# A unit of token work on TensorE ahead of the sums of the step before, in a two-layer attention kernel

## Chip, cores and metric

The kernel runs on 1 core of one Trainium2 chip. The metric is device time in microseconds (us); the time before is a median of 3 runs.

## The reference

What is computed is a chain of two transformer layers on x of shape (4, 1024, 128), all in fp32, each sublayer with a residual and a layernorm without weights behind it:

- layer 0: attention with 16 heads of 8, q and k normalised over the whole row of 128 and divided by sqrt(8), scores divided by a temperature per head, softmax over all 1024 keys, projection with bias; then a linear layer with inputs quantised to int8 per row.
- layer 1: attention with 16 heads of 8, a layernorm per head on q and k, rotary embedding, a causal mask, softmax, projection with bias; then a gated MLP with 384 hidden units: down(silu(gate) * up).

```python
attn = softmax(q @ k.T / temperature); out = (attn @ v) @ proj_w.T + proj_b
x = layernorm(x + out)
x = layernorm(x + quantised_matmul(x, weight_q) * weight_scale + bias)
scores = where(tril, scale * q @ k.T, -inf); out = softmax(scores) @ v @ Wo.T + bo
x = layernorm(x + out)
x = layernorm(x + (silu(x @ wg.T) * (x @ wu.T)) @ wd.T)
```

## The kernel before, in words

The queries are cut into 8 chunks of 512 tokens (4 batches, two halves) per layer. A pass is one chunk and one group of 4 heads; there are 64 passes, two passes make a pair, and the 4 passes (two pairs) of a chunk together fill `attn`. A pass is cut into steps of 128 keys (`STEPS`, 400 of them; in layer 1 keys behind the mask are left out and remainders of two passes share a step).

In every step the attention engines do this:

- TensorE, scores (`scores`, L885): two blocks of 2 heads each, transposed scores of 128 keys by 512 queries; each block fills two banks of `ps`. There are three such slots, so block k waits until ScalarE has read block k-3.
- ScalarE (L757): an exponential of each block into `probs` (128x1024). GpSimd zeroes what the causal mask takes (L673, `mask`).
- TensorE, sums (`sums`, L907): probs times v, all four heads side by side in bank `ACC`, together with a row of ones that gives the denominators. They accumulate over both passes of a pair.
- at the end of a pair VectorE turns the bank (`whole_chunk`, "turn": L1151, L1154, L1155) into `heads_t`; at the end of a chunk it transposes `heads_t` into `attn` (L1158).

Beside it runs the token work: everything of the layers that isn't attention, cut into pieces. Its TensorE pieces are the *units*: `qkv` (L853), `qkT` and `normT` and `xqT` (transposes, L779), `ffn` (L848), `proj` (L838), `gate` and `up` (L860), `down` (L864). All write the one bank `SIDE` (`stage`), and VectorE reads each (`read`) before the next may start. A unit also waits for its own input: `proj` for `attn` (`attn_ready`), others for results of VectorE. The VectorE pieces stand between the reads. A planner (`side_order`) that runs when the kernel is built writes for every step which unit and which VectorE pieces belong to it (`SIDE_ORDER`); at most one unit stands in a step, 200 of the 202 units stand in steps that this change can touch. The planner estimates TensorE's and VectorE's time with fixed prices and supposes that the unit comes behind the sums, except in the pending steps (below). `proj` stands 3 steps behind the last step of its chunk.

TensorE's order in step s (`steps` in the TensorE block, L960 on) is: scores of blocks 2s+3 and 2s+4, then the sums of step s-1, then the unit of step s. TensorE executes in program order. One kind of step is different, the *pending* step: if step s-1 is the first of a pair, its sums overwrite the bank that VectorE is turning, so the unit goes first and these sums come behind it. The step before it (s-1 is the last of a pair) holds the sums that the turn waits for.

SyncE issues the DMAs (parts of q and k out to `parts_scratch`, L540; rows back into `q_st` and `k_st`, L522) in an order of its own that comes from the same schedule; GpSimd copies v into `v_st` (L655). ScalarE also does a tanh for each gate unit, two steps behind it.

Of the kernel before, what the change touches and what calls it, by code (L numbers as in the profile page):

```python
# [85 lines left out]
STEPS = []  # L86
# [6 lines left out]
STEPS = [(*x, FIRST[x[0]] == s, LAST_STEP[x[0]] == s) for s, x in enumerate(STEPS)]  # L93
# [271 lines left out]
def program(nc, a, ctx):  # L365
# [408 lines left out]
    def _(pe):  # L774
# [93 lines left out]
        def scores(k, shifted):  # L868

            s, tiles_ = k // 2, STEPS[k // 2][1]  # L870
            for p in dict.fromkeys(x[0] for x in tiles_):
                if k % 2 == 0 and FIRST[p] == s:
                    pe.wait_ge(rows_in[p % KB], 32 * (p // KB + 1) + (32 * PRODUCTS - 32 if p % KB == 0 else 0))
                    if shifted:
                        shifts(p)
            if k % 2 == 0 and tiles_[0][0:2] == (0, TC):
                pe.wait_ge(more_rows_in, 16 * PRODUCTS)
            if k >= SLOTS:

                pe.wait_ge(probs_ready, k - SLOTS + 1)  # L880
            for p, kt, lo, at, n in tiles_:
                for e in range(2):
                    h = k % 2 * 2 + e
                    row = slice(h * HR, (h + 1) * HR)
                    last_ = mm(slot(k)[:, e, at:at + n], k_st[row, p % KB, kt * P:(kt + 1) * P],  # L885
                               q_st[row, p % KB, lo:HALF], start=True, stop=not shifted)
                    if shifted:
                        row = slice(h * HR, h * HR + PARTS)
                        last_ = mm(slot(k)[:, e, at:at + n], ones_st[row, :], shift_st[row, p % 2, lo:HALF], start=False, stop=True)
            last_.then_inc(scores_ready, 1)  # L890

        def sums(s):
            _, tiles_, w, m, _, _ = STEPS[s]
            for p in dict.fromkeys(x[0] for x in tiles_):
                if FIRST[p] == s:
                    pe.wait_ge(v_in, p + 1)
                    if p and p % 2 == 0:
                        pe.wait_ge(sums_turned, p // 2)
            if tiles_[0][0:2] == (0, TC):
                pe.wait_ge(more_v_in, 1)  # L900
            if m:
                pe.wait_ge(masked, MASKED[s])
            else:
                pe.wait_ge(probs_ready, 2 * s + 2)
            for x, (p, kt, lo, at, n) in enumerate(tiles_):
                for h in range(GH):
                    last_ = mm(acc[HR * h:HR * (h + 1), lo:HALF], v_st[:, p % VB, kt, h, :],  # L907
                               probs[:, (2 * s + h // 2) % PS, h % 2, at:at + n], start=FIRST[p] == s and p % 2 == 0 and x == 0,
                               stop=LAST_STEP[p] == s and p % 2 == 1 and x == len(tiles_) - 1, skip_group_check=True)
            last_.then_inc(sums_ready, 1)  # L910
# [25 lines left out]
        def keep_warm(n, bank):  # L936
            for _ in range(n):
                mm(ps[:, bank, :], warm[:, 0:P], warm[:], start=True, stop=True)
# [21 lines left out]
        def steps(shifted):  # L960
            if shifted:
                for name, c, e, what, k in FIRST_KEYS:
                    if e == "pe":
                        stage(name, c, what, k)

            pe.wait_ge(parts_ready["prep"], 2)
            for k in range(SLOTS):
                scores(k, shifted)
            if not shifted:
                stage("prep", 1, "qkT", 1)  # L970
            for s in range(NS + 1):
                for k in (2 * s + 3, 2 * s + 4):
                    if k < 2 * NS:
                        scores(k, shifted)
                if s < 2 and not shifted:
                    keep_warm(WARM[4], ACC)
                pending = s > 1 and STEPS[s - 1][4] and STEPS[s - 1][0] % 2 == 0
                if s and not pending:
                    sums(s - 1)
                for name, c, e, what, k in SIDE_ORDER[s]:  # L980
                    if e == "pe" and (name, c, e, what, k) != FIRST_KEYS[0] and \
                            not (shifted and (name, c, e, what, k) in FIRST_KEYS):
                        stage(name, c, what, k)
                if s and pending:

                    sums(s - 1)
            end()

        with pe.If(far_scores < 1):
            steps(False)  # L990
        with pe.Else():
            steps(True)
# [437 lines left out]
```

## Time and profile before

| | |
|---|---|
| median of 3 runs | 862.54 us (862.50 to 862.57) |
| the profiled execution's own time | 866.08 us |
| its span, first to last instruction | 864.4 us |
| granted TensorE clock, mean | 0.989 |
| TensorE, ScalarE, VectorE, GpSimd busy | 96%, 89%, 64%, 17% |
| HBM | 51.0 MB read, 35.7 MB written |

The profile's records are of one execution. PE is TensorE's matmuls, PEld its weight loads, ACT ScalarE, DVE VectorE, POOL GpSimd, SPq SyncE's DMA issues; L with a number is a line of the kernel. A matmul's recorded end is modelled, and consecutive matmuls overlap, so lengths on TensorE are best read from start to start.

### The profile page before, as it was taken

Reading aid. Unit: us, or ns where it says so; the run is one execution under the profiler, and the core shown is the slowest. Engines: PE = TensorE matmul, PEld = TensorE weight load, DVE = VectorE, ACT = ScalarE, POOL = GpSimd, SP = SyncE. Lnnn points to the kernel's source line nnn. Section 1 sums busy time; section 2 is a strip of 40 time slices with the busy share of each in tenths; the row PEclk is TensorE's granted clock in tenths of the full one; section 3 lists DMA queues with packets and bytes.
Section 4 is the critical chain, followed back from the end, with each engine's and each line's share of the span. In section 5 each row is a group of like instructions: output and inputs, shape, how many; then the busy total and the mean of one; then the engine's idle time right before and its main releaser. Section 6 shows DMA issues by size and latency. Waiting matters only on the chain.

```text
span 864.4 us, 16509 instructions
## 1 busy us (share of the span) xinstructions
PE 831.2 (96%) x6266; PEld 307.4 (36%) x6268; DVE 550.9 (64%) x1459; ACT 771.8 (89%) x864; POOL 150.1 (17%) x352
## 2 busy tenths in 40 slices
PE   8899999999999899999999999999999999989995
PEld 4232333333333333333333433343333443434444
DVE  6264666668758567787672576765563476765656
ACT  4899999999999799899899999999999998979851
POOL 3000000000001400034100410023200442352210
PEclk9999999999999899999999999999999999989998
DMA  5755513314432611352340321142140330062000
GB/s 152 246 160 184 171 38 115 105 37 158 161 122 76 218 38 61 111 184 74 134 160 25 111 98 38 61 160 74 38 159 25 98 112 25 26 221 85 1 13 27
DMA packets 48565, 88.60 MB, mean 103 GB/s; under 512 B 5088, under 2 KB 14432, under 8 KB 48480
## 3 DMA queue, kind: packets, MB, share of 16 engines
q1 hardware_dynamic: 48000, 87.00, 29.9%
q8 instruction: 52, 0.85, 0.4%
q10 hardware_dynamic: 480, 0.48, 0.2%
q14 instruction: 33, 0.27, 0.1%
HBM read 51.03 MB, written 35.65 MB: 100 GB/s over the span
## 4 chain that ended last, share of the span: by engine, by line
PE 80%; DVE 11%; DMA 3%; issue 3%; SPq 2%; ACT 1%; POOL 1%; DVEq 0%; ACTq 0%; POOLq 0%
PE ps L907 39%; PE ps L885 24%; PE ps L853 5%; PE ps L864 3%; PE ps L860 3%; PE ps L779 3%; DMA q_st<-parts_scratch 2%; PE ps L838 2%; ACT probs L757 1%; DVE th L1310 1%; DVE hT L1311 1%; SPq L540 1%; DVE sums_t L1151 1%; DVE mid_part L1300 1%; DVE mid_part L1301 1%
## 5 line engine op out<-in xcount | busy, mean ns | idle before, releaser
L757 ACT ACTIVATE probs<-ps 128x1024 f32<-128x1024 f32 x800 | 751.7, 1073 | 58.3 <-PE ps L885 55.6
L907 PE MATMUL ps<-probs,v_st 128*32 128x512 f32 (+3 forms) x3584 | 430.4, 562 | 3.4 <-issue 1.2
L885 PE MATMUL ps<-q_st,k_st 32*128 32x512 f32 (+3 forms) x1792 | 269.7, 462 | 7.8 <-DMA q_st<-parts_scratch 5.2
L885 PEld LDWEIGHTS ps<-q_st,k_st 32*128 32x128 f32 x1792 | 123.7, 184 | 251.1 <-ACT probs L757 157.4
L673 POOL TENSOR_SCALAR_AFFINE_SELECT probs<-probs 128x256 f32<-128x256 f32 x256 | 108.6, 444 | 152.1 <-ACT probs L757 150.7
L907 PEld LDWEIGHTS ps<-probs,v_st 128*32 128x32 f32 x3584 | 76.4, 109 | 112.1 <-issue 79.3
L655 POOL COPY v_st<-v_all 128x256 f32<-128x256 f32 (+1 forms) x65 | 28.3, 437 | 404.4 <-PE ps L907 396.5
L1151 DVE STREAM_TRANSPOSE sums_t<-ps 128x512 f32<-128x512 f32 x32 | 22.9, 716 | 44.0 <-PE ps L907 43.5
L1285 DVE COPY mid_qkv<-ps 128x384 f32<-128x384 f32 x32 | 17.8, 558 | 38.4 <-PE ps L853 35.6
L860 PE MATMUL ps<-yTp,w_hid 128*128 128x512 f32 x84 | 30.8, 448 | 4.4 <-DVE hT L1311 1.5
L1285 DVE COPY prep_qkv<-ps 128x384 f32<-128x384 f32 x24 | 13.4, 558 | 30.9 <-PE ps L853 30.8
L853 PE MATMUL ps<-w_qkv,yT 128*128 128x384 f32 x64 | 29.2, 538 | 0.0
L864 PEld LDWEIGHTS ps<-w_down,hT 128*128 128x128 f32 x168 | 20.8, 191 | 23.3 <-issue 16.5
L1262 DVE TENSOR_TENSOR x_all<-ps,x_all 128x512 f32<-128x512 f32 x15 | 10.4, 692 | 26.9 <-PE ps L838 26.9
L864 PE MATMUL ps<-w_down,hT 128*128 128x128 f32 x168 | 26.2, 292 | 1.2 <-DVE last_y L1315 0.8
L1305 DVE COPY gate_sb<-ps 128x512 f32<-128x512 f32 x21 | 14.5, 691 | 18.6 <-PE ps L860 18.5
L1315 DVE TENSOR_TENSOR last_y<-ps,last_y 128x128 f32<-128x128 f32 x24 | 7.0, 292 | 30.0 <-PE ps L864 29.7
L860 PEld LDWEIGHTS ps<-yTp,w_hid 128*128 128x128 f32 x84 | 12.5, 188 | 35.2 <-issue 12.8
L1310 DVE SCALAR_TENSOR_TENSOR th<-th,gate_sb 128x512 f32<-128x512 f32 x21 | 14.7, 701 | 15.9 <-PE ps L860 15.6
L853 PE MATMUL ps<-w_qkv,xT 128*128 128x384 f32 x48 | 21.9, 538 | 0.7
L1300 DVE CAST mid_part<-ps 128x512 fp32r<-128x512 f32 x18 | 12.4, 692 | 15.2 <-PE ps L779 14.1
L838 PE MATMUL ps<-w_out,attn 128*128 128x128 f32 x120 | 17.2, 286 | 2.8 <-DVE attn L1158 2.6
(188 smaller groups left out, 634.0 us busy)
## 6 DMA issues: line engine op xcount, KB each, us to landing
k_st<-parts_scratch SPq DMA_DIRECT2D x47, 512.0 KB, 3.5
parts_scratch<-mid_part SPq DMA_DIRECT2D x36, 512.0 KB, 3.9
q_st<-parts_scratch SPq DMA_DIRECT2D x63, 256.0 KB, 4.2
parts_scratch<-prep_part SPq DMA_DIRECT2D x28, 512.0 KB, 4.0
k_st<-parts_scratch SPq DMA_DIRECT2D x16, 256.0 KB, 2.8
xT<-in_xT SPq DMA_DIRECT2D x8, 256.0 KB, 5.0
x_all<-in_x SPq DMA_DIRECT2D x8, 256.0 KB, 5.6
out<-yo SPq DMA_DIRECT2D x7, 256.0 KB, 2.4
```

What stands on the lines that cost most here:

```text
L655: return g_.tensor_copy(v_st[:, p % VB, t, :, p % 2 * SR:p % 2 * SR + D], v_all[:, layer, b % 2, t, g * GH * D:(g + 1) * GH * D] .rearrang ...
L673: op = g_.affine_select(out=block_, in_=block_, compare_op=ALU.is_ge, fill=0.0, base=0, pattern=[[0, 2], [1, P]], channel_multiplier=-1)
L757: nc.scalar.activation(probs[:, k % PS, :, 0:w], slot(k)[:, :, 0:w], ACT.Exp).then_inc(probs_ready, 1)
L779: last_ = tp(dst[:, t * P:(t + 1) * P], src(t), idn[:])
L838: last_ = mm(side[:, t * P:(t + 1) * P], attn[:, t * P:(t + 1) * P], w_out[:, layer, :], start=True, stop=True)
L853: last_ = mm(side[:, 0:3 * C], src[:, k * P:(k + 1) * P], w_qkv[:, 0 if name == "prep" else 1, :], start=True, stop=True)
L860: last_ = mm(side, w_hid[:, 0 if what == "gate" else 1, k * P:(k + 1) * P], yTp[:, n, :], start=(n == 0), stop=(n == PARTS - 1))
L864: last_ = mm(side[:, k * P:(k + 1) * P], hT[:, j, k * P:(k + 1) * P], w_down[:, j * P:(j + 1) * P], start=(j == 0), stop=(j == NJ - 1))
L885: last_ = mm(slot(k)[:, e, at:at + n], k_st[row, p % KB, kt * P:(kt + 1) * P], q_st[row, p % KB, lo:HALF], start=True, stop=not shifted)
L907: last_ = mm(acc[HR * h:HR * (h + 1), lo:HALF], v_st[:, p % VB, kt, h, :], probs[:, (2 * s + h // 2) % PS, h % 2, at:at + n], start=FIRST[ ...
L1151: v.transpose(sums_t[:], acc).then_inc(sums_turned, 1)
L1285: v.tensor_copy(job[name]["qkv"][:, k, :], side[:, 0:3 * C]).then_inc(side_read, 1)
```

## The change

Only the order in TensorE's steps changes. Before, the sums of step s-1 went ahead of the unit, except in a pending step. Now the unit goes ahead of the sums, except where step s-1 is the last of a pair (`STEPS[..][5]` is set for the last step of a pass, and the pass number is odd), and in step 1. The pending steps keep the order that they had. The planner, with its supposition on the order, and the lists of all other engines stay as they are.

```diff
-                pending = s > 1 and STEPS[s - 1][4] and STEPS[s - 1][0] % 2 == 0
-                if s and not pending:
+                first = s > 1 and STEPS[s - 1][5] and STEPS[s - 1][0] % 2 == 1
+                if s == 1 or first:
                     sums(s - 1)
                 for name, c, e, what, k in SIDE_ORDER[s]:
                     if e == "pe" and (name, c, e, what, k) != FIRST_KEYS[0] and \
                             not (shifted and (name, c, e, what, k) in FIRST_KEYS):
                         stage(name, c, what, k)
-                if s and pending:
-
+                if s > 1 and not first:
                     sums(s - 1)
```

## Rows read from the trace of the kernel before

**Rows 1.** Page, part 1: busy time of the engines.
```profile
PE 831.2 (96%) x6266; PEld 307.4 (36%) x6268; DVE 550.9 (64%) x1459; ACT 771.8 (89%) x864; POOL 150.1 (17%) x352
```

**Rows 2.** Page, part 5: groups; busy and mean, then idle time before, with releaser.
```profile
L757 ACT ACTIVATE probs<-ps 128x1024 f32<-128x1024 f32 x800 | 751.7, 1073 | 58.3 <-PE ps L885 55.6
...
L860 PE MATMUL ps<-yTp,w_hid 128*128 128x512 f32 x84 | 30.8, 448 | 4.4 <-DVE hT L1311 1.5
...
L838 PE MATMUL ps<-w_out,attn 128*128 128x128 f32 x120 | 17.2, 286 | 2.8 <-DVE attn L1158 2.6
```

**Rows 3.** Timeline of TensorE: start, length, line; sums, gate unit, sums of two steps.
```profile
790.56 1.06 PE L907 MATMUL ps<-probs,v_st 128*32 128x512 f32 x8
791.56 0.73 PE L860 MATMUL ps<-yTp,w_hid 128*128 128x512 f32 x2
...
792.66 1.07 PE L907 MATMUL ps<-probs,v_st 128*32 128x256 f32 x16
```

**Rows 4.** Timeline of TensorE: the unit of a pending step, then the next step.
```profile
335.43 0.73 PE L860 MATMUL ps<-yTp,w_hid 128*128 128x512 f32 x2
...
337.52 1.06 PE L907 MATMUL ps<-probs,v_st 128*32 128x512 f32 x8
```

**Rows 5.** Timeline: VectorE's copy of a qkv unit and the next qkv unit.
```profile
253.30 0.56 DVE L1285 COPY mid_qkv<-ps 128x384 f32<-128x384 f32 x1 [1.65 <-PE ps L853]
...
254.63 0.91 PE L853 MATMUL ps<-w_qkv,yT 128*128 128x384 f32 x2
```

**Rows 6.** Timeline around the projection of the third chunk of layer 0.
```profile
218.38 1.07 PE L907 MATMUL ps<-probs,v_st 128*32 128x512 f32 x8
...
219.43 0.71 DVE L1158 STREAM_TRANSPOSE attn<-heads_t 128x512 f32<-128x512 f32 x1 [0.50 <-DVE mid_part L1301]
...
220.29 1.13 PE L838 MATMUL ps<-w_out,attn 128*128 128x128 f32 x8 [0.84 <-DVE attn L1158]
...
221.89 1.02 ACT L757 ACTIVATE probs<-ps 128x1024 f32<-128x1024 f32 x1 [1.24 <-PE ps L885]
```

**Rows 7.** Timeline: four other projections, for the last also the sums and `attn`.
```profile
93.35 1.16 PE L838 MATMUL ps<-w_out,attn 128*128 128x128 f32 x8 [0.17 <-DVE prep_part L1301]
...
373.52 1.13 PE L838 MATMUL ps<-w_out,attn 128*128 128x128 f32 x8 [0.19 <-DVE attn L1158]
...
425.41 1.13 PE L838 MATMUL ps<-w_out,attn 128*128 128x128 f32 x8 [0.46 <-DVE attn L1158]
...
571.25 1.06 PE L907 MATMUL ps<-probs,v_st 128*32 128x512 f32 x8
571.40 0.71 DVE L1158 STREAM_TRANSPOSE attn<-heads_t 128x512 f32<-128x512 f32 x1
```

**Rows 8.** Timeline: `attn` and the sums behind the scores at another projection.
```profile
154.36 0.71 DVE L1158 STREAM_TRANSPOSE attn<-heads_t 128x512 f32<-128x512 f32 x1
...
155.23 1.07 PE L907 MATMUL ps<-probs,v_st 128*32 128x512 f32 x8
```

**Rows 9.** Timeline of TensorE: two projections and the scores' waits behind them.
```profile
283.39 1.13 PE L838 MATMUL ps<-w_out,attn 128*128 128x128 f32 x8 [0.71 <-DVE attn L1158]
...
290.77 0.50 PE L885 MATMUL ps<-q_st,k_st 32*128 32x256 f32 x4 [2.68 <-DMA q_st<-parts_scratch]
...
760.52 1.13 PE L838 MATMUL ps<-w_out,attn 128*128 128x128 f32 x8 [0.41 <-DVE attn L1158]
...
763.45 0.79 PE L885 MATMUL ps<-q_st,k_st 32*128 32x512 f32 x2 [1.38 <-DMA q_st<-parts_scratch]
```

**Rows 10.** Timeline: a copy of VectorE behind a pending step, and a unit that waits.
```profile
339.36 0.69 DVE L1305 COPY gate_sb<-ps 128x512 f32<-128x512 f32 x1 [0.51 <-PE ps L860]
...
343.17 0.73 PE L860 MATMUL ps<-yTp,w_hid 128*128 128x512 f32 x2 [0.46 <-DVE prep_part L1301]
```

**Rows 11.** Stretches: length, then PE, PEld, DVE, ACT, POOL busy, granted clock, DMA share, GB/s.
```profile
763.20:770.00 6.80, 6.55 (x44) 2.30 (x48) 1.53 (x7) 3.49 (x4) 2.69 (x7) 0.50 0.85 316
...
224.00:230.80 6.80, 6.79 (x52) 2.05 (x48) 6.03 (x29) 6.80 (x8) 0.00 (x0) 1.00 0.34 117
```

## The prediction

> **What bounds the kernel now.** I read the share of busy time first, then the groups with their idle time, then the order of time on each engine around single steps. TensorE shows 96% busy [rows 1], but its records also cover time in which scores wait for a place, so the share alone does not tell the limit. ScalarE's 800 exponentials come to 751.7 us with 58.3 us idle, of which 55.6 are waits for scores [rows 2]. So two engines alternate as the limit: where a step has no token unit, ScalarE; where it has one, TensorE. A TensorE-bound step with a gate unit takes 792.66 - 790.56 = 2.10 us from sums to sums [rows 3]; ScalarE's two exponentials take 751.7 / 400 steps = 1.88 us [rows 2]. ScalarE gets its next scores only when TensorE has finished both sums and unit, so what counts is the length of scores + sums + unit, in whatever order, and every wait inside it.
>
> **The change, part by part.** The schedule has 200 token units. In 13 the step behind it ends a pair (sums stay in front), in 6 the step is the pending one, in which the unit already stood in front. 181 units move ahead of one block of sums. Nothing is added or removed; the planner's lists for VectorE, SyncE and GpSimd are the same, so no queue of theirs is reordered.
>
> *Length of a step with another order.* The pending steps show the new order already: unit at 335.43, next unit position (there, sums) at 337.52, 2.09 us for the same gate unit [rows 4] against 2.10 in the old order [rows 3]. Difference 0.01 us; over some 125 steps in which TensorE is the limit, between -1.3 and +1.3 us. I take 0.
>
> *Units that follow each other.* Where unit follows unit, the one behind waits for VectorE's copy of the one ahead. The copy of the qkv unit starts at 253.30 and takes 0.56, the next unit starts at 254.63, 0.77 us later than it could [rows 5]. The unit moves ahead by a block of sums (1.00 us, from 790.56 to 791.56 [rows 3]) and so does the one before it, and with it the copy: the distance is unchanged. Cost 0. The same holds for a unit behind a chain of VectorE work, if that chain starts from a moved unit.
>
> *Units whose input does not come earlier.* This is where the change costs. The projection reads `attn`, which comes from the turn of the pair's sums; those sums stay in front, so `attn` comes when it came before, but the projection now is reached one block of sums sooner, and the sums are queued behind its wait. Before, that block covered part of the wait. At the third chunk of layer 0 the sums start at 218.38, `attn` is ready at 219.43 + 0.71 = 220.14, the projection starts at 220.29 after TensorE idled 0.84 us although the sums had run [rows 6]. After the change nothing runs until 220.29 and then the sums come: + 1.00 us. ScalarE idles 1.24 us here already [rows 6], so it has no store of scores and the 1.00 us goes to the end of the kernel in full. The projections at 93.35, 373.52 and 425.41 also start after an idle time (0.17, 0.19, 0.46) [rows 7], so each loses the whole cover, 1.00 us. At 571.25 the sums start and `attn` is ready at 571.40 + 0.71 = 572.11 [rows 7]: 0.86 us. Together 4 x 1.00 + 0.86 = 4.86 us.
>
> Two more projections waited, at 283.39 and 760.52. Soon after them the scores wait for rows by DMA, 2.68 us and 1.38 us [rows 9], and these transfers follow the q parts of a chunk, whose unit stands in a step that ends a pair and does not move. The extra 1.00 us vanishes in that wait: cost 0, and 1.00 us each if the transfer turns out to hang on the delayed scores. The other 8 of the 15 projections find `attn` ready: as at 154.36 + 0.71 = 155.07, where the scores are done at 155.23, the start of what follows them [rows 8]. Cost 0 (0.05 us each at most).
>
> *One chain that comes only half as much sooner.* Behind the pending step at 335.43 VectorE works off the turn, a copy and a reduction; the next copy, at 339.36, comes after only 0.51 us of idleness [rows 10], so it and the chain behind it can come only 0.51 us sooner, while the unit that ends the chain (at 343.17, after a wait) has lost 1.00 us of cover: 1.00 - 0.51 = 0.49 us.
>
> *What could be gained.* A unit in the step that ends a pair stays behind the sums while its predecessor comes 1.00 us earlier. One such unit waited, some 0.4 us, but the unit behind it waits for the turn; I take 0. Later sums free `probs` and `v_st` later: both have steps of reserve; I take 0. The sums' wait for the mask gets more room only in steps with a unit; there are few of those in the masked passes, and I take 0.
>
> Sum: 4.86 + 0.49 = 5.35 us. The profiled execution took 866.08 us, so it would take 871.4; the unprofiled median is 862.54, and since all terms are differences between records of the same run I add them there: **867.9 us** (+0.6%).
>
> **Rivals.**
> *The clock falls at the longer waits.* At 763.2 to 770.0 the granted clock was 0.50, the 1.2 GHz level, right after TensorE had waited 0.41 and then 1.38 us [rows 9, 11]. After the change the wait at 220.29 would be 0.84 + 1.00 = 1.84 us. In the slow stretch ScalarE is busy 3.49 of 6.80 us, against 6.80 of 6.80 in a stretch without units at full clock [rows 11]: up to 3.3 us for one fall, so 871.2 us; two falls 874.5. Against it: the wait at 220.29 stands alone, with full work before and behind. The Trainium skill (TensorE: Matmul & The Clock Gate, section "Why this matters for your kernels") asks only that gaps longer than any wait of rows 9 be avoided. By that rule the clock would not fall here and the sum stays at 867.9; the fall in rows 11 speaks against the rule. Chance 0.17.
>
> *Units come sooner and VectorE's waits go (faster).* Place: the units of gate, up and projection, before which TensorE idles 4.4 and 2.8 us [rows 2]. If VectorE, fed a block of sums sooner, has each unit's input ready when TensorE arrives, both go: 862.5 - 7.2 = 855.3 us; half of it gives 859. It decides from the point where inputs come at least as much sooner as the unit. For it: VectorE is idle before most of its copies (1.65 us before that of a qkv unit [rows 5]). Against it: the input comes sooner by exactly as much as the unit, never more, save in the 13 steps that end a pair; and `attn` does not come sooner at all. Chance 0.08.
>
> *It does nothing that can be measured.* If ScalarE had scores in store at the projections, the extra wait would be hidden, and the time stays 862.5. Against it stands ScalarE's idle time at 221.89. Chance 0.12.
>
> *The covers I trusted fail.* The two projections before the DMA waits count 1.00 us each, the order costs 0.01 us per step: 5.35 + 2.0 + 1.3 = 8.65, 871.2 us. It belongs to the upper part of my range. Chance 0.13.
>
> **How the numbers follow.** The forecast itself has 0.50, the rivals 0.17, 0.08, 0.12 and 0.13. A measurement of this kernel can tell 0.2% (1.7 us) from no change. Slower by more than that: 0.50 + 0.17 + 0.13 + 0.01 = 0.81; within it 0.11; faster 0.08. The range leaves out the faster rival, the lower half of no change and two falls of the clock: 863.5 to 872.5 us.
>
> **What the profile would show.** Right: idle time of TensorE before the projection matmuls (L838) of some 2.8 + 6 = 8 to 9 us in place of 2.8, with 7 long waits, the longest near 1.8 us; next to it nothing changed in idle time before gate, up and qkv units; the sequence scores, unit, sums, 2.09 us per gate step; ScalarE's wait for scores up by about 5 us. The scores at 290.77 still wait for DMA, by some 1 us less. Wrong: if the projections' idle time rises but the time does not (it was hidden); if idle time appears before other units, then their inputs did not come sooner and I undercounted; if a stretch besides the two known ones shows clock 0.5; or if steps with units differ from 2.1 us.

## The result, and the profile after

The changed kernel's median is 869.42 us over 20 runs (864.83 to 873.2). Beside it on the same chips the kernel before had 865.48 (20 runs, 862.5 to 869.59). The ratio, chip by chip, is 1.0033 with a 95% interval of 1.0017 to 1.0049: slower by 2.9 us (1.5 to 4.2). The forecast of 867.9 had been counted from the 862.54 of the first three runs, which lie at the low end of the 20; as a difference it said 5.35 us, and that is about 2.4 us too much. (The two medians themselves lie 3.9 us apart; chip by chip it is 2.9.) That 867.9 came so near to 869.42 is in part luck: the start was 2.9 us too low and the difference 1.4 to 2.4 us too large, and the two errors offset each other. So the sign was right and the range held, and most of what follows asks where the 2.4 us are. The profiled execution took 869.39 us, its span is 867.6.

The page of the kernel after, parts 1 and 5 (most helpers' line numbers are one lower than before):

```profile
PE 830.8 (96%) x6266; PEld 309.2 (36%) x6268; DVE 550.2 (63%) x1459; ACT 770.3 (89%) x864; POOL 149.1 (17%) x352
...
L757 ACT ACTIVATE probs<-ps 128x1024 f32<-128x1024 f32 x800 | 750.3, 1073 | 63.1 <-PE ps L885 60.3
...
L860 PE MATMUL ps<-yTp,w_hid 128*128 128x512 f32 x84 | 30.8, 447 | 4.2 <-DVE gate_sb L1304 1.4
L853 PE MATMUL ps<-w_qkv,yT 128*128 128x384 f32 x64 | 29.2, 538 | 0.0
L838 PE MATMUL ps<-w_out,attn 128*128 128x128 f32 x120 | 18.7, 304 | 10.8 <-DVE attn L1157 9.7
```

Apart from the weight loads (309.2 us against 307.4) no engine works longer than before. TensorE now idles 10.8 us before the projections in place of 2.8, ScalarE 63.1 us before its exponentials in place of 58.3 [rows 2]. Before gate, up and qkv units nothing was added: 4.2 us before gate and up, where it was 4.4, so the faster rival, by which those waits go, did not come. These are the signs that the prediction named for being right; one of its signs of being wrong, new stretches at clock 0.5, is there too (below).

The timeline of TensorE in the kernel after, gate units in two steps (start, length, group):

```profile
792.03 0.74 PE L860 MATMUL ps<-yTp,w_hid 128*128 128x512 f32 x2
792.69 1.06 PE L907 MATMUL ps<-probs,v_st 128*32 128x512 f32 x8
...
794.12 0.73 PE L860 MATMUL ps<-yTp,w_hid 128*128 128x512 f32 x2
794.78 1.06 PE L907 MATMUL ps<-probs,v_st 128*32 128x512 f32 x8
```

A gate step takes 794.78 - 792.69 = 2.09 us, against 2.10 [rows 3]. The order of scores, unit and sums is worth 0.01 us here. Over all steps with the same unit in both kernels the medians from the end of one step's scores to the end of the next one's are: qkv 2.28 us before and after, gate 2.10 and 2.10, up 2.10 and 2.10, down 2.30 and 2.30.

The projection of [rows 6] in the kernel after, timeline of TensorE, VectorE and ScalarE:

```profile
218.16 0.72 PE L885 MATMUL ps<-q_st,k_st 32*128 32x512 f32 x4
...
219.86 0.71 DVE L1157 STREAM_TRANSPOSE attn<-heads_t 128x512 f32<-128x512 f32 x1 [0.50 <-DVE mid_part L1300]
...
220.72 2.05 PE L838 MATMUL ps<-w_out,attn 128*128 128x128 f32 x8 [1.84 <-DVE attn L1157]
222.69 1.67 PE L907 MATMUL ps<-probs,v_st 128*32 128x512 f32 x8
...
224.83 1.94 ACT L757 ACTIVATE probs<-ps 128x1024 f32<-128x1024 f32 x2 [3.76 <-PE ps L885]
```

The wait before the projection is 1.84 us, exactly 0.84 + 1.00. But then the projection takes 2.05 us in place of 1.13 and the sums 1.67 in place of 1.07: the clock fell. ScalarE waits 3.76 us where it waited 1.24.

The granted clock in stretches of the kernel after (start:end, length, PE, PEld, DVE, ACT, POOL busy, clock, DMA share, GB/s):

```profile
220.50:223.90 3.40, 3.18 (x16) 1.98 (x16) 1.10 (x4) 0.58 (x1) 0.00 (x0) 0.51 0.80 299
374.10:377.50 3.40, 3.40 (x16) 1.58 (x15) 1.34 (x5) 0.64 (x1) 0.41 (x1) 0.51 0.38 142
766.70:770.10 3.40, 3.40 (x34) 1.52 (x30) 2.49 (x14) 0.94 (x2) 0.20 (x1) 0.50 1.04 396
292.10:298.90 6.80, 5.50 (x70) 2.65 (x74) 3.99 (x15) 6.37 (x8) 4.37 (x13) 1.00 0.59 210
```

And of the kernel before, the stretches that answer to the first two and the last:

```profile
292.20:299.00 6.80, 6.59 (x54) 2.69 (x54) 6.08 (x19) 4.56 (x6) 3.51 (x9) 0.50 0.36 118
...
220.20:223.60 3.40, 3.31 (x28) 1.84 (x32) 1.94 (x8) 2.16 (x3) 0.00 (x0) 1.00 1.00 379
373.50:376.90 3.40, 3.38 (x38) 2.28 (x38) 1.47 (x6) 2.81 (x4) 0.81 (x2) 1.00 0.73 250
```

Besides the stretches at the very end, the kernel before ran at the 1.2 GHz level (0.50) for 6.8 us at 292.2 and for 6.8 us at 763.2 [rows 11]. The kernel after does so for 3.4 us each at 220.5, 374.1 and 766.7. Two falls of the clock are new, behind waits of 1.84 and 1.38 us for `attn`; behind those of 1.71 us at 286.31 and 1.43 us at 427.88 there is none. A long fall is gone and another halved. The stretch at 292 runs at full clock now. The granted clock is even higher after: its median over the 20 runs is 0.991, against 0.987 over the 35 runs of the kernel before in the first set of experiments below.

The reason that 292 is level stands in TensorE's timeline of the kernel after:

```profile
286.31 1.13 PE L838 MATMUL ps<-w_out,attn 128*128 128x128 f32 x8 [1.71 <-DVE attn L1157]
...
292.89 0.50 PE L885 MATMUL ps<-q_st,k_st 32*128 32x256 f32 x4 [0.97 <-DMA q_st<-parts_scratch]
```

The projection before it waits 1.71 us (0.71 before), and the scores' wait for the transferred rows has shrunk from 2.68 us [rows 9] to 0.97. The delay is swallowed by the DMA wait, as forecast. I had said "by some 1 us less"; it is 1.7 us.

I then compared the two profiled executions step by step: the time at which the scores of a step end, and by how much the distance of the two kernels changes from one step to the next. The steps with a change of over 0.2 us at the projections: +0.90 (first), +2.52 (at 220.72), +0.76 (286.31), +2.77 (373.93), +0.97, +0.98, and +0.24, +0.25, +0.24, +0.20 at four projections of which I had expected nothing. There are others of this size away from the projections; they are taken up further down.

### The profile page after: what moved, and what is told of

It is laid out like the page before. It is cut to its first block, busy times and chain, and to the rows that moved or that the text cites. A ratio compares the mean times of both kernels' runs of the same rounds, so it can differ in the third digit from the quotient of the medians.

```text
span 867.6 us, 16509 instructions
## 1 busy us (share of the span) xinstructions
PE 830.8 (96%) x6266; PEld 309.2 (36%) x6268; DVE 550.2 (63%) x1459; ACT 770.3 (89%) x864; POOL 149.1 (17%) x352
## 4 chain that ended last, share of the span: by engine, by line
PE 80%; DVE 14%; DMA 2%; issue 2%; SPq 1%; ACT 1%; DVEq 0%; ACTq 0%; POOL 0%
PE ps L907 40%; PE ps L885 23%; PE ps L853 5%; PE ps L779 3%; PE ps L860 3%; PE ps L864 3%; PE ps L838 2%; DVE sums_t L1150 1%; DMA q_st<-parts_scratch 1%; DVE heads_t L1154 1%; DVE th L1309 1%; DVE hT L1310 1%; DVE attn L1157 1%; SPq L540 1%; DVE rd L1153 1%
## 5 line engine op out<-in xcount | busy, mean ns | idle before, releaser
L757 ACT ACTIVATE probs<-ps 128x1024 f32<-128x1024 f32 x800 | 750.3, 1073 | 63.1 <-PE ps L885 60.3
L673 POOL TENSOR_SCALAR_AFFINE_SELECT probs<-probs 128x256 f32<-128x256 f32 x256 | 110.4, 451 | 150.8 <-ACT probs L757 148.9
L655 POOL COPY v_st<-v_all 128x256 f32<-128x256 f32 (+1 forms) x65 | 25.8, 398 | 424.5 <-PE ps L907 416.6
L838 PE MATMUL ps<-w_out,attn 128*128 128x128 f32 x120 | 18.7, 304 | 10.8 <-DVE attn L1157 9.7
L838 PEld LDWEIGHTS ps<-w_out,attn 128*128 128x128 f32 x120 | 15.9, 207 | 14.4 <-issue 7.7
```

The costliest lines, as they stand in the source:

```text
L655: return g_.tensor_copy(v_st[:, p % VB, t, :, p % 2 * SR:p % 2 * SR + D], v_all[:, layer, b % 2, t, g * GH * D:(g + 1) * GH * D] .rearrang ...
L673: op = g_.affine_select(out=block_, in_=block_, compare_op=ALU.is_ge, fill=0.0, base=0, pattern=[[0, 2], [1, P]], channel_multiplier=-1)
L757: nc.scalar.activation(probs[:, k % PS, :, 0:w], slot(k)[:, :, 0:w], ACT.Exp).then_inc(probs_ready, 1)
L838: last_ = mm(side[:, t * P:(t + 1) * P], attn[:, t * P:(t + 1) * P], w_out[:, layer, :], start=True, stop=True)
```

## The experiments

Eleven further runs. The kernel before ran beside each set of them, 35, 35 and 29 times, with medians of 866.37, 866.45 and 866.33 us, so absolute times of the three sets can be set side by side to some tenths.

**The changed kernel again**, with no edit, as the yardstick of the first set.

> The changed kernel again, so that the next three have it on the same chip. Both theories: 2 to 5 us slower than the kernel before. Theory A (the projections lose the cover of their sums, 5 times 0.86 to 1.00 us): idle time before the projection matmuls about 10.8 us against 2.8. Theory B (the loss is made by the TensorE clock, which falls at the longer waits): the time goes with the granted clock; a run with clock 0.995 takes some 865 us, one with 0.988 some 872.

Measured: 869.28 us, ratio 1.0034 (1.0011 to 1.0058). Idle time before the projections is 10.8 us again; the falls of the clock stand at 222.8, 287.7 and 376.4. Two of three places are those of the first profile. The third is not, so which of the long waits is followed by a fall varies between executions.

**Only the projections go back behind the sums.**

```diff
                 first = s > 1 and STEPS[s - 1][5] and STEPS[s - 1][0] % 2 == 1
+                first = first or any(x[3] == "proj" for x in SIDE_ORDER[s])
```

> The changed kernel, but in the 15 steps with a projection the sums go first again. Theory A: the whole loss goes, within 1 us of the kernel before; idle time before the projections back at about 2.8 us. Theory B says the same of the total, since the long waits go too; what is left over would be the price of the other 166 moved units, which I hold to be 0 (-1 to +1 us). If the time stays 2 us or more above the kernel before, both theories are wrong and the other units cost something.

Measured: 867.65 us, ratio 1.0016 (0.9994 to 1.0038); 3.1 us of idle time before the projections, as before the change. So by the medians half of the loss goes (869.28 to 867.65), and 1.3 us stay, where I had expected at most 1; the interval of the ratio holds anything from no loss to more than the whole of it, so the steps have to tell. Step by step against the kernel before, the gains stay (-0.56 and -0.51 us at two steps), but there are new losses: +0.75, +0.42, +0.74, +0.43, +0.60 and +0.92 us, each one to five steps behind a projection (of the 0.60, 0.40 stand in the changed kernel too). At all six stands a transposition or a feed-forward unit. VectorE and TensorE at the first of them, in this kernel:

```profile
306.97 0.69 DVE L1262 TENSOR_TENSOR x_all<-ps,x_all 128x512 f32<-128x512 f32 x1 [2.35 <-PE ps L838]
...
309.07 0.43 DVE L1204 TENSOR_SCALAR xq<-mid_y 128x512 bf16<-128x512 f32 x1
...
309.70 0.38 PE L779 MATMUL ps<-ident_b,xq 128*128 128x128 bf16 x4 [0.72 <-DVEq L1205]
```

The unit at 309.70 belongs to another chunk than the projection, and `xq` is not computed from it. But in VectorE's program the work on `xq` stands behind the reading of the projection (L1262), for which VectorE waits 2.35 us. The projection comes as late as before, so `xq` does too (2.10 us behind the reading, 2.09 in the kernel before: 307.73 to 309.82), while its unit has moved ahead of its sums. I read the six as the same loss one unit further on; the last experiment below tests that.

**Only the projections move.** The kernel before, with this added:

```diff
                 pending = s > 1 and STEPS[s - 1][4] and STEPS[s - 1][0] % 2 == 0
+                pending = pending or any(x[3] == "proj" for x in SIDE_ORDER[s])
```

> The kernel before, with only the 15 projections moved ahead of their sums. Theory A: the whole loss of the change comes back, 2 to 5 us slower than before, idle time before the projections about 11 us. Rival (other moved units cost): less than half of the loss.

Measured: 870.07 us, ratio 1.0031 (1.001 to 1.0052). The loss with the 15 projections alone, 3.7 us by the medians and 0.31% by the ratio, is as large as that of the whole change (2.9 us, 0.34%). The page of this kernel:

```profile
L757 ACT ACTIVATE probs<-ps 128x1024 f32<-128x1024 f32 x800 | 750.6, 1071 | 65.3 <-PE ps L885 62.5
...
L838 PE MATMUL ps<-w_out,attn 128*128 128x128 f32 x120 | 17.8, 293 | 10.5 <-DVE attn L1159 9.3
```

The idle time before the projections is that of the changed kernel (10.5 against 10.8), ScalarE idles 65.3 us. The other 166 moved units together cost nothing that this comparison can tell; step by step some of them lose and some gain, as is shown further down.

**The changed kernel with its long waits filled.** Ahead of its wait for `attn`, the projection issues 3 to 5 matmuls on constant data at six places; their output is not used.

```diff
+    FILLERS = {11: 5, 15: 4, 23: 5, 27: 4, 39: 3, 55: 4}
...
+                for _ in range(FILLERS.get(k, 0)):
+                    mm(side, warm[:, 0:P], warm[:], start=True, stop=True)
                 pe.wait_ge(attn_ready, k // GB + 1)
```

> The changed kernel with 3 to 5 matmuls of zeros (bf16, 512 columns) into the side bank ahead of six of the waiting projections, within their idle time. Nothing waits less. Theory B: the falls at the projections go, the granted clock rises by 0.002 to 0.004 in the mean and the time falls by 1.5 to 4 us against the changed kernel. Theory A: the step behind each projection is as late as in the changed kernel, so at equal clock nothing is gained, 0 to 1 us either way.

Measured: 865.79 us, ratio 0.9996 (0.9978 to 1.0014). No wait and no dependency was taken away; TensorE only does unused work while it waits, and 3.5 us go. TensorE's timeline at the projection of [rows 6] in this kernel:

```profile
217.82 0.72 PE L888 MATMUL ps<-q_st,k_st 32*128 32x512 f32 x4
219.31 1.03 PE L838 MATMUL ps<-warm 128*128 128x512 bf16 x4 [0.77 <-DVE mid_part L1303]
220.29 1.16 PE L841 MATMUL ps<-w_out,attn 128*128 128x128 f32 x8
221.38 1.06 PE L910 MATMUL ps<-probs,v_st 128*32 128x512 f32 x8
```

The projection starts when `attn` is there, at 220.29, but it and the sums behind it take 1.16 and 1.06 us, not 2.05 and 1.67. The mean clock rises from 0.991 to 0.994, with no fall left in the profiled execution before 851 us. This is the cost of the falls in the changed kernel, 869.28 - 865.79 = 3.5 us, and the remaining time is that of the new order alone.

**The kernel before with its DMA waits filled**, the same remedy at the places where the old order has its falls:

```diff
+    ROW_FILLERS = {1: 3, 19: 8, 58: 5}
...
+                if k % 2 == 0 and FIRST[p] == s and p in ROW_FILLERS and not shifted:
+                    pe.wait_ge(probs_ready, k - SLOTS + 1)
+                    for _ in range(ROW_FILLERS[p]):
+                        mm(slot(k)[:, 0, :], warm[:, 0:P], warm[:], start=True, stop=True)
```

> The kernel before, with matmuls of zeros (3, 8 and 5) into a free score slot while TensorE waits for rows by DMA in three places (near 37, 290 and 763 us). Nothing waits less. If the falls of the clock that the kernel before shows behind these waits cost it some 2.5 us in the mean (my reading of 0.987 against 0.991), the mean clock rises to 0.991 or more and the median falls by 1.5 to 3 us. If the falls cost nothing on the path, the time stays within 0.7 us.

Measured: 862.27 us, ratio 0.9954 (0.9936 to 0.9972). TensorE's timeline in this kernel at the wait of [rows 9]:

```profile
287.64 1.90 PE L876 MATMUL ps<-warm 128*128 128x512 bf16 x8
290.23 0.50 PE L890 MATMUL ps<-q_st,k_st 32*128 32x256 f32 x4 [0.70 <-DMA q_st<-parts_scratch]
```

The rows come when they came before, and the falls at 292 and 763 are gone: with what the fillers near 37 us prevent (the profiles of three of these kernels have a fall there), they cost the kernel before 866.45 - 862.27 = 4.2 us. (One fall of 3.4 us, at 25.4 us, is in this profile and not in the second one of the same kernel, further down.) With the falls behind the long waits taken out on both sides, the new order costs 865.79 - 862.27 = 3.5 us, or 3.1 by the second measurement of this kernel; with them, it costs 2.9, because its own falls take 3.5 in place of 4.2.

**The projections one step later** in the changed kernel (and the units behind them with them):

```diff
-            if g == GB - 1 and LAST_STEP[p] + 3 == s:
+            if g == GB - 1 and LAST_STEP[p] + 4 == s:
```

> The changed kernel, the projections planned 4 steps behind the last step of their chunk instead of 3. attn is then ready when TensorE arrives. Theory A (the cover of the projections is the whole price): idle time before the projections falls from 10.8 to under 2 us and the kernel is 3 to 5 us faster than the changed one, level with or faster than the kernel before by up to 2 us. Rival (the token chain, planned with sums first, becomes late elsewhere): less than 2 us are won back.

Measured: 869.47 us, ratio 1.0024 (1.0005 to 1.0042). The idle time before the projections falls from 10.8 to 0.6 us and the time does not: the theory's 3 to 5 us are not there, and the rival's "less than 2" is met. TensorE's timeline at the scores' waits for rows, and two stretches with their clock, in this kernel:

```profile
292.90 0.50 PE L885 MATMUL ps<-q_st,k_st 32*128 32x256 f32 x4 [2.32 <-DMA q_st<-parts_scratch]
...
771.95 0.79 PE L885 MATMUL ps<-q_st,k_st 32*128 32x256 f32 x4 [3.50 <-DMA q_st<-parts_scratch]
```

```profile
293.90:297.30 3.40, 3.20 (x26) 0.95 (x18) 2.29 (x6) 2.43 (x3) 1.83 (x5) 0.50 0.19 51
771.80:778.60 6.80, 6.42 (x44) 2.53 (x48) 3.47 (x12) 3.29 (x4) 2.28 (x6) 0.50 0.56 197
37.90:44.70 6.80, 6.65 (x24) 1.48 (x24) 1.43 (x4) 3.11 (x4) 0.00 (x0) 0.50 0.64 223
```

The waits have become DMA waits, with longer falls behind them (mean clock 0.987). The waits for rows from `parts_scratch` come to 6.3 us in all, against 2.1 in the changed kernel. So what the edit saves at the projections it gives back, 4.2 us of it in these waits and the rest, I think, in the clock behind them. At one granted clock, 0.991, it takes 866.1 us (2 runs) where the changed kernel takes 869.4 (9 runs), but such a comparison shows little: at 0.991 the kernel before and the changed one lie 5.5 us apart in the first set (863.8 and 869.3), the filled versions 3.5, since falls at different places do not cost the same. The split between waits and clock is not shown.

**The planner told of the new order**, on top of the last edit: it counts the sums (1.0 us) behind the unit in place of ahead of it, and allows more lateness for a unit (`LATE` 2.5 for 1.5).

```diff
-        if pending:
+        ahead = s > 1 and not ends_pair(s - 1)
+        if ahead:
...
+        elif ahead:
+            pe += 1.0
```

> As the run before, and the planner's clock is told that units stand ahead of the sums (one of its limits, LATE, is 2.5 instead of 1.5, without which it finds no complete plan). Theory A: the same as with the projections a step later alone, within 1 us, since units that follow each other keep their distance. Rival (units arrive too soon everywhere): faster than that by over 1.5 us.

Measured: 865.58 us, ratio 0.9984 (0.9966 to 1.0003). My theory, the time of the run before within 1 us, missed; the rival's "faster by over 1.5 us" is met with 3.9 us. No projection waits for VectorE, and the waits for rows are 1.42 to 2.01 us, with three falls of 6.8 us or less behind them. They still come to 5.3 us. Which of the planner's other choices brings the rest no run takes apart.

**Both kinds of waits filled** in the changed kernel, the two edits above together:

```diff
+    ROW_FILLERS = {1: 3, 19: 8, 58: 5}
+    FILLERS = {11: 5, 15: 4, 23: 5, 27: 4, 39: 3, 55: 4}
```

> The changed kernel with both sets of filling matmuls (projections and rows). The clock should fall nowhere inside the kernel (granted clock 0.995 or more in all runs), and what is left against the kernel before with its rows filled is the bare price of the changed order: 5.4 us by the sum of the prediction (4.9 of it at the projections).

Measured: 867.86 us, ratio 1.0026 (1.0004 to 1.0049), at the same clock (0.994) as with the projections' fillers alone. That is 5.6 us above the filled kernel before, next to the 5.4 that I expected, but by luck: 867.86 - 865.79 = 2.1 us of it come with the second set of fillers and are no price of the order. It is a miss of mine: the numbers of fillers fit the DMA waits of the kernel before, and in the changed kernel those are shorter. Step by step against the version with the projections' fillers alone, +0.67 and +1.17 us stand at the two DMA waits. A filler costs its own time where the wait is not long enough for it.

**The kernel before with filled waits again**, as the yardstick of the third set.

> The kernel before with the three waits for the weight rows filled by matmuls on warm data, once more, as the yardstick on this chip. Expected 862.3 us (0.995 to 0.996 of the kernel before), granted clock 0.994, as in its first run; if the gain was chance of that chip, it lies at 0.998 or above.

Measured: 862.73 us, ratio 0.9977 (0.9955 to 0.9999), 12 runs. (The rows waited for are those of q and k, not weights.) By the medians the gain is 0.4% again; by the ratio it is 0.2% here and 0.5% in the second set, and the intervals of the two overlap.

**The planner's version with the waits for rows filled.**

```diff
+    ROW_FILLERS = {1: 3, 19: 8, 59: 8}
```

> The changed kernel with its projections a step later, the planner told of the new order, and the waits for the weight rows filled. It tells whether the new order can beat the old one once the late units are planned for. Theory (the new order costs 0.00 to 0.01 us a step by itself, its loss is only late units and clock): without the falls of the clock it gains 2 to 3.5 us on 865.6, so 862 to 863.5, mean clock 0.993 or more. Rival (what the moved projections left is a cost of the order or of the planner's other choices, and the clock is level elsewhere): it stays within 1 us of 865.6.

Measured: 862.13 us, ratio 0.9952 (0.9931 to 0.9972); mean clock 0.994. TensorE's groups in this kernel:

```profile
L893 PE MATMUL ps<-q_st,k_st 32*128 32x512 f32 (+3 forms) x1792 | 270.7, 459 | 1.4 <-ACT probs L761 0.9 <-DMA q_st<-prep_part 0.3 <-DMA q_st<-parts_scratch 0.2
...
L842 PE MATMUL ps<-w_out,attn 128*128 128x128 f32 x120 | 17.4, 288 | 0.0
```

No wait is left before the projections and 0.5 us for rows. The theory's 862 to 863.5 is met and the rival's 865.6 is not: the falls were worth 865.58 - 862.13 = 3.5 us here. One long wait is left, 2.37 us before a transposition at 754.9, with a fall of 3.4 us behind it. The new order, planned for, reaches the old one (862.73 on the same chip) and does not pass it by anything that can be told. Both beat the kernel before and the changed one.

**Sums last only where no projection, no feed-forward unit and no transposition of a norm or of quantised rows stands** (the `qkT` transpositions do move), with the waits for rows filled:

```diff
+                pending = s > 1 and STEPS[s - 1][4] and STEPS[s - 1][0] % 2 == 0
+                first = first or not pending and any(x[3] in ("proj", "xqT", "ffn", "normT") for x in SIDE_ORDER[s])
...
+    ROW_FILLERS = {1: 3, 19: 8, 58: 5}
```

> The sums stay in front of the units at every step that has a projection, a feed-forward unit or one of the transposed norm and query units, and go last only at steps with the other units (the query, key and value units above all), with the waits for the weight rows filled. It tells whether the gains of the new order come from the qkv units alone. Theory (the gain of 0.55 us at step 196 is a qkv copy that comes a block sooner; the losses all sit behind projections, which this order covers again): 861.5 to 862.5 us, 0 to 0.8 us below the yardstick of this chip, and no idle of more than 3.5 us in all ahead of the projections. Rival (late units behind an unmoved unit lose their cover, as they did where only the projection steps were put back): 863 to 864.5 us.

Measured: 867.03 us, ratio 1.0009 (0.999 to 1.0029), 4.3 us above the yardstick of its chip, at a level clock. My theory fell, and the rival's 863 to 864.5 was too low also. TensorE's waits in this kernel (what waits, for whom, us in all, times, longest):

```profile
PE ps L839 <- DVE attn L1164: 3.0, 5, 0.9
PE ps L854 <- DVE yT L1275: 2.6, 7, 0.4
PE ps L861 <- DVE yTp L1273: 2.4, 3, 1.1
```

The projections are as in the kernel before. But seven qkv units now wait for the transposed norm, where in the kernels before and after no such wait stands (0.0 us), and gate units for theirs. The transpositions stay behind their sums, the qkv and gate units that read them have moved ahead of theirs: each loses its cover. Step by step that is +0.38 to +0.50 us at seven qkv units and +1.0 at two gate units. The gain of 0.56 us is there as well, and drowned.

## Why the prediction was right, and where its sum was off

**The five uncovered projections: right.** Step by step, filled version of the changed kernel against filled version of the kernel before, so with no fall behind the long waits on either side, they come to 0.89, 0.93, 1.13, 0.90 and 0.91 = 4.76 us. The prediction had 4.86. The runs with the projections alone moved, and alone put back, show it from both sides: what costs is the unit that is reached a block sooner while its input is not. With 1.00 us each for four of them the prediction was right to 0.13 us at worst.

**Equal order, equal distance of following units: right.** 2.09 against 2.10 us in a gate step, no new idle time at qkv, gate and up. The reason given for it (both units move, so the distance stays) is what the two failed mixed orders show by its breach: put back only some of the units and those behind them wait.

**The chain behind the pending step: right in kind, half in size.** The forecast was 0.49 us for the unit at 343.17. Its step costs 0.28 us between the two profiles and 0.25 between the filled versions; TensorE waits 0.75 us before it (at 342.61 in the kernel after) in place of 0.46. The sum took the turn to come when it came before. Measured against TensorE's steps, which are 0.16 us later in the kernel after, the turn comes 0.24 us sooner (335.12 against 335.20), since VectorE is free before it, and the copy 0.72 us sooner (338.80 against 339.36), not 0.51: 1.00 - 0.72 = 0.28 us.

**Two late units that the prediction does not list.** A transposition of the norm, at 717.56 in the kernel after, now waits 0.40 us; its step costs +0.41. Its chain starts from a moved unit, so by the rule above it should keep its distance, but from the first aggregation to the last operation it takes 716.24 - 713.36 = 2.88 us, in the kernel before 711.93 - 709.45 = 2.48. Small operations of VectorE that took 0.16 us there take 0.32 where GpSimd's mask now runs beside them (at 714.93 and 715.29, the mask from 714.84 to 715.61). And a `qkT` transposition at 62.15 waits 0.20 us and costs +0.24.

**"The other 8 of the 15 projections find `attn` ready ... Cost 0 (0.05 us each at most)": wrong.** Four of them pay 0.25, 0.25, 0.23 and 0.21, 0.94 us together. TensorE's and VectorE's timeline of the kernel before and after at one of them:

```profile
486.72 0.71 DVE L1158 STREAM_TRANSPOSE attn<-heads_t 128x512 f32<-128x512 f32 x1
...
487.31 1.07 PE L907 MATMUL ps<-probs,v_st 128*32 128x384 f32 x16
488.31 1.16 PE L838 MATMUL ps<-w_out,attn 128*128 128x128 f32 x8
```

```profile
490.16 0.71 DVE L1157 STREAM_TRANSPOSE attn<-heads_t 128x512 f32<-128x512 f32 x1
...
490.18 0.63 PE L885 MATMUL ps<-q_st,k_st 32*128 32x512 f32 x6
491.02 1.13 PE L838 MATMUL ps<-w_out,attn 128*128 128x128 f32 x8 [0.21 <-DVE attn L1157]
```

`attn` is ready at 490.16 + 0.71 = 490.87, 0.06 us after the scores are done (490.18 + 0.63), the first matmul starts 0.15 us behind it, and TensorE idles 0.21 us. In the kernel after, 14 of the 15 projections start 0.15 us after the recorded end of `attn`; the same distance stands in [rows 6], 220.29 - 220.14. I had looked at the one of [rows 8], which had 155.23 - 155.07 = 0.16 us to spare and costs nothing, and took it for all eight. The trace of before had the difference: at four of the eight `attn` is ready 0.22 to 0.23 us before the recorded end of the scores, at the other four 0.03 to 0.06 us after it, as at 487.43 above.

**"The extra 1.00 us vanishes in that wait": right, and more than that.** The steps at the two DMA waits of the filled versions end up 0.9 us better, not equal (+0.81, then -1.41; and -0.33). Part of that may be the row fillers of the one side, since the filled versions differ in them there; I leave the split open. The rival by which both covers fail did not come.

**"What could be gained ... I take 0", three times: wrong.** Together about -1.7 us: -0.55 and -0.53 us at two steps, -0.20, -0.19, -0.24 at three others. The -0.53 us are the first of the prediction's three points, the unit that stands in a step that ends a pair and had waited: its predecessor comes sooner, and the turn that I held against it did not stop it. The largest, -0.55, is the mask, the last of the three. The timeline of GpSimd and TensorE in the kernel before:

```profile
416.46 0.61 POOL L650 COPY v_all<-mid_qkv 128x512 f32<-128x512 f32 x1 [5.21 <-DVEq L1288]
...
417.02 1.75 POOL L673 TENSOR_SCALAR_AFFINE_SELECT probs<-probs 128x256 f32<-128x256 f32 x2
...
418.83 1.07 PE L907 MATMUL ps<-probs,v_st 128*32 128x512 f32 x8 [0.63 <-POOL probs L673]
```

and in the kernel after:

```profile
418.44 0.61 POOL L650 COPY v_all<-mid_qkv 128x512 f32<-128x512 f32 x1 [4.23 <-DVEq L1287]
...
419.00 1.75 POOL L673 TENSOR_SCALAR_AFFINE_SELECT probs<-probs 128x256 f32<-128x256 f32 x2
...
421.12 1.07 PE L907 MATMUL ps<-probs,v_st 128*32 128x512 f32 x8
```

GpSimd copies the `v` parts ahead of a mask that ends at 417.02 + 1.75 = 418.77, and the sums wait 0.63 us for it. After the change the qkv unit, and so the copy and the mask, come a block of sums sooner in their step while these sums come later in theirs: the mask ends at 419.00 + 1.75 = 420.75, and the sums that need it start at 421.12, with no wait. I had dismissed this with "there are few of those in the masked passes". There is one, and it was idle time that the trace of before showed.

**The clock: the rival was in part true, and its price was wrong.** Falls came at 220.5 and 374.1, behind single waits of 1.84 and 1.38 us with full work around them, against my argument that such a wait "stands alone". By the Trainium skill (TensorE: Matmul & The Clock Gate, section "Why this matters for your kernels") only gaps longer than these two need be avoided; by that rule these two falls would not be there, and this trace does not agree. At their steps the distance of the kernels grows by 2.52 and 2.77 us, of which 1.0 is cover (0.93 and 1.13 by the filled versions), so a fall costs 1.5 to 1.8 us and not the 3.3 that I took from a stretch twice as long [rows 11]. And I did not count the other side: the kernel before pays 4.2 us for its own falls, the changed one 3.5, so on balance the clock gave 0.7 us back.

The sum by what was measured, order alone: 4.76 + 0.94 + 0.25 + 0.41 + 0.24 and 0.16 (a step next to a gain), - 0.93 at the DMA waits, - 1.71 gains, = 4.1 us. The medians of the filled versions say 3.5, or 3.1 with the second measurement of the kernel before; each of their ratios is known to 0.2%, some 1.6 us, so they do not contradict the 4.1. Less 0.7 for the clock the steps give 3.4 us; measured were 2.9 (1.5 to 4.2). The filled profiles also differ by 0.8 us in their first steps. That is no part of the change: it stands ahead of 38.2 us, where the first unit that changed place comes. The kernel before with fillers has the fall at 25.4 us there in its first profile; in its second it has none, and the difference is 0.4. In the 13 traces these steps end anywhere between 36.9 and 38.8 us.

The terms that failed are thus the gains set at 0 and the clock, in one direction, and the just-late waits and the two unlisted units in the other. They cancel in part, and that a forecast of 5.35 us for a difference of 2.9 is not further off owes something to that.

## What to carry to other kernels

Moving a unit ahead of other work costs nothing in itself; what it costs is the cover of its wait, and, but for the 0.41 us above, it cost that only where the input does not move along. So list, for each moved unit, whether its producer moves too, and whether what stands ahead of the producer in its engine's order does. Here an input had to be ready 0.15 us before the unit's new start; later ones cost the rest. Price a new idle stretch of TensorE with its consequences for the granted clock, on both sides of the comparison: matmuls on constant data in TensorE's longest waits, no longer in all than the wait, gave the kernel before 4.2 and 3.6 us here, more than the change took.

## What the runs showed of the hardware that I had not expected

The granted clock fell to the 1.2 GHz level behind TensorE waits of 1.38, 1.84, 2.3 and 2.7 us, and behind others (1.71 us at 286.31, 1.43 us at 427.88) it did not in the same execution. In the second profile of the changed kernel there is a fall behind the 1.71 us. A fall lasted 3.4 or 6.8 us. Two executions of one kernel have them at partly different places, and most of the spread between runs goes with that: the changed kernel took 865.0 us at a mean clock of 0.995 (3 runs), 869.4 at 0.991 (9) and 872.0 at 0.988 (2); the kernel before, in the first set, 862.5 at 0.993 (2 runs) and 866.4 at 0.987 (13 runs). Matmuls on constant data in the waits removed the falls behind them in both kernels and were worth 3.5 us in the changed one and 4.2 and 3.6 us in the one before, without any dependency changed.

A projection whose input comes late starts 0.15 us after the recorded end of VectorE's operation, at 14 of 15 places. Small VectorE operations took 0.32 us in place of 0.16 where GpSimd's mask ran beside them.
